# Two graph attention layers on one core: the first layer in seven row groups of 1024 and two of 512 instead of sixteen of 512

## The reference

```python
h = jnp.maximum(_layernorm(x, axis=-1), 0.0)
Wh = h @ W                                  # layer 1: h @ W.T
e = leaky_relu((Wh @ a1)[:, None] + (Wh @ a2)[None, :])     # slope 0.2
scores = jnp.where(adj > 0, e, -9e15)
x = x + elu(softmax(scores, axis=1) @ Wh)
```

## Time and profile before

| | us |
|---|---|
| median of the runs | 1394.34 |
| profiled execution | 1393.29 |
| its span on the core | 1391.6 |
| VectorE, ScalarE, TensorE busy | 1231.1, 1188.9, 1154.9 |

### The profile page before, as it was taken

How to read it: one execution, slowest core, us unless ns; L and a number is a source line. 1 busy time by engine, 2 the same in 40 slices (tenths; PEclk the granted TensorE clock), 3 DMA queues, 4 the chain that set the end, 5 groups by cost and what they waited for, 6 DMA issues and landing times.

```text
span 1391.6 us, 52932 instructions
## 1 busy us (share of the span) xinstructions
PE 1154.9 (83%) x20824; PEld 1121.6 (81%) x20824; DVE 1231.1 (88%) x2210; ACT 1188.9 (85%) x1826; POOL 312.8 (22%) x520
## 2 busy tenths in 40 slices
PE   2726989888898998998898660999899989999996
PEld 2525989888888898898898540999899989999996
DVE  6787889988999898999897778989899999998996
ACT  2346999999899999999999536799899989998995
POOL 2342454444444444444420000000000000000000
PEclk9857999999999999999999875999999999999998
DMA  9998999999999999999972100000101010110000
GB/s 157 168 209 148 212 198 208 212 211 189 211 204 212 211 210 211 209 211 211 210 142 55 27 2 32 2 25 2 33 2 32 2 33 8 27 33 2 17 2 24
DMA packets 128133, 157.09 MB, mean 113 GB/s; under 512 B 59280, under 2 KB 59408, under 8 KB 128016
## 3 DMA queue, kind: packets, MB, share of 16 engines
q0 software_dynamic: 73728, 134.25, 52.3%
q1 hardware_dynamic: 54288, 21.11, 6.9%
HBM read 285.25 MB, written 4.26 MB: 208 GB/s over the span
## 4 chain that ended last, share of the span: by engine, by line
PE 33%; issue 24%; DVE 19%; ACT 15%; DMA 8%; ACTq 1%; DVEq 1%; POOL 1%; POOLq 0%; SPq 0%
PE psum L1210 30%; ACT toggle L558 11%; DMA stream<-in_adj_dram 6%; DVE work L933 5%; DVE work L969 3%; DVE toggle L964 3%; ACT stream L575 2%; DVE stream L706 2%; PE psum L1105 2%; DVE toggle L946 1%; PE psum L1191 1%; DMA x_scratch<-y_tile 1%; ACT sums L575 1%; DVE work L813 1%; POOL stream L643 0%
## 5 line engine op out<-in xcount | busy, mean ns | idle before, releaser
L1210 PE MATMUL psum<-parts_d,toggle 128*128 128x130 f16 x8192 | 983.3, 223 | 40.6 <-DVE work L969 40.4
L1210 PE MATMUL psum<-parts_g,work 128*128 128x130 f16 x8192 | 983.1, 222 | 0.0
L1210 PEld LDWEIGHTS psum<-parts_d,toggle 128*128 128x128 fp8e4 x8192 | 804.7, 98 | 45.7 <-issue 45.3
L1210 PEld LDWEIGHTS psum<-parts_g,work 128*128 128x128 fp8e4 x8192 | 811.1, 99 | 5.6 <-issue 2.3
L558 ACT ACTIVATE toggle<-s_row,steep_d 128x512 uint8 (+1 forms) x952 | 590.8, 724 | 1.2 <-issue 0.2
L558 ACT ACTIVATE toggle<-stream,steep_d 128x1024 uint8<-128x1024 f32 x416 | 440.7, 1158 | 38.4 <-PE psum L1210 37.7
L643 POOL DMA_DIRECT2D stream<-in_adj_dram x512 | 311.5, 610 | 382.7 <-DVE stream L706 320.5
L964 DVE TENSOR_TENSOR toggle<-work,toggle 128x1024 int32<-128x1024 int32 x256 | 312.3, 1220 | 62.2 <-ACT toggle L558 59.2
L969 DVE TENSOR_TENSOR work<-work,toggle 128x1024 int32<-128x1024 int32 x256 | 311.7, 1218 | 0.7
L706 DVE TENSOR_SCALAR stream<-stream 128x1024 bf16<-128x1024 bf16 x512 | 201.8, 421 | 38.2 <-DMA stream<-in_adj_dram 30.9
L1105 PE MATMUL psum<-pack_w,stream 128*128 128x8 bf16 x4096 | 132.5, 166 | 73.4 <-DVE stream L706 68.6
(11 more groups left out here) (121 smaller groups left out, 361.7 us busy)
## 6 DMA issues: line engine op xcount, KB each, us to landing
stream<-in_adj_dram POOLq DMA_DIRECT2D x512, 256.0 KB, 7.6
s_row<-s_scratch SPq DMA_DIRECT2D x16, 256.0 KB, 6.1
stream<-s_scratch SPq DMA_DIRECT2D x8, 512.0 KB, 4.3
toggle<-in_x_dram SPq DMA_DIRECT2D x4, 512.0 KB, 6.9
x_tile<-in_x_dram SPq DMA_DIRECT2D x16, 128.0 KB, 10.6
x_scratch<-y_tile SPq DMA_DIRECT2D x16, 128.0 KB, 9.5
stream<-x_scratch SPq DMA_DIRECT2D x4, 512.0 KB, 5.4
stream<-x_scratch SPq DMA_DIRECT2D x8, 256.0 KB, 4.5
```

Of the source, the lines that this page charges most:

```text
L1210: ins = nc.tensor.matmul(psum[:, bank, COLS[third]:COLS[third + 1]], mask.bitcast(FP8), parts[e][:, t, :, :].rearrange("p k h -> p (k h)") ...
```

## The change

The first layer is cut into 7 groups of 1024 rows in 16 chunks, shaped as in the second layer, and 2 groups of 512 at its end. The code calls the three shapes K = 0, 1, 2. In the groups of 1024 ScalarE makes all four signs of a chunk; in the first small group VectorE takes one in every second chunk, in the second one in every chunk. 72 steps instead of 56 are converted ahead of the first group. The first six groups have 4 conversions a chunk as before, the seventh has 2 a chunk (32), the first small group 4 in each of its first six chunks (24). The sixteen pieces of a large group fill six PSUM banks and the words move to banks 6 and 7; no bank has a twin in K = 0, and the two small groups use three banks each. `take_sums` stands after chunk 2 everywhere. The tiles `s_row`, `sums`, `x_tile`, `y_tile` and `rden` are shared by both layers, and the total, tanh and exp tiles are parts of `sums`; so `take_sums` waits until y of the group before is written (`y_ready`), where it waited for the second step of the epilogue. `move` is cut in two, so that the load of a row of s can stand between. The code of the fallback for extreme inputs, which does not run here, is adapted.

```diff
-    GTS = (4, 8)
-    CTS = (8, 4)
+    GTS = (8, 4, 8)
+    LAYER_OF = (0, 0, 1)
+    COUNTS = (7, 2, 8)
+    CTS = (4, 8, 4)
-    AHEAD = 6 * PACE
+    AHEAD = 8
+    PACK_BANK = 6
...
-        return [s for s in range(AHEAD + c * PACE, AHEAD + (c + 1) * PACE) if s < limit]
+    def steps_at(K, g, c):
+        if K == 0 and isinstance(g, int) and g == COUNTS[0] - 1:
+            return list(range(AHEAD + 2 * c, AHEAD + 2 * c + 2))
+        if K == 0:
+            return list(range(AHEAD + c * PACE, AHEAD + (c + 1) * PACE))
+        if K == 1 and g == 0 and c < 6:
+            return list(range(AHEAD + 32 + c * PACE, AHEAD + 32 + (c + 1) * PACE))
+        return []
...
+    def own_tiles(K, g, c):
+        if K == 0:
+            return 0
+        if K == 1:
+            return int(g == 1 or c % 2 == 1)
+        return int(c % 4 != 3)
...
-                        for s in range(28 + 7 * i, 35 + 7 * i):
+                        for s in range(28 + 11 * i, 39 + 11 * i):
                             convert(0, s)
...
-                act.wait_ge(sums_free, g + (L * LGROUPS[0] + 1))
+                if not (isinstance(g, int) and gg == 0):
+                    act.wait_ge(y_ready, gg)
...
+                for c in range(CHUNKS[K]):
+                    signs(K, g, c, slot)
+                    for k in words_at(K, g, c):
+                        store_words(base_of(K, g), k)
+                    if before:
+                        if c == 2:
+                            take_sums(*before)
+                        if c == (13 if K != 1 else 6):
+                            tanh(*before[0:2])
...
+                        back = 2 if K == 2 and (bank < OWN_BANKS or bank >= 6) else 1
+                        pe.wait_ge(bank_free, g * BIG + (BEFORE[K] - (back - 1) * BIG + last_in_bank(K, bank, side) + 1))
```

More of the change, by code:

```diff
@@ L64, in gat2_kernel @@
     BLOCK = CTS[0] * GTS[0] * P
-    LAYER = (0, LGROUPS[0] * CHUNKS[0])
+    BIG = 8
     WPT = P // BITS
@@ L105, in own_tiles @@
[L105 to L120, removed]
@@ new lines, in own_tiles, with own_up_to, chunk @@
+    def own_tiles(K, g, c):
+        if K == 0:
+            return 0
+        if K == 1:
+            return int(g == 1 or c % 2 == 1)
+        return int(c % 4 != 3)
+    def own_up_to(K, g, c):
+        here = sum(own_tiles(K, g, k) for k in range(c + 1))
+        first = sum(own_tiles(1, 0, k) for k in range(CHUNKS[1]))
+        if K == 1:
+            return g * first + here
+        return g * sum(own_tiles(2, 0, k) for k in range(CHUNKS[2])) + (first + CHUNKS[1] + here)
+    def chunk(K, g, c):
+        return g * CHUNKS[K] + (CHUNK0[K] + c)
@@ L139, in gat2_kernel, with where, last_in_bank @@
+    def where(K, r, e, side):
+        q = 2 * r + e
+        if K == 1:
+            return 3 * side + q // 3, q % 3
+        if K == 2 and q < 3 * OWN_BANKS and side:
+            return q // 3 + 6, q % 3
+        return q // 3, q % 3
+    def last_in_bank(K, bank, side):
+        return max(r for r in range(GTS[K]) if bank in (where(K, r, 0, side)[0], where(K, r, 1, side)[0]))
     with ExitStack() as ctx:
@@ L586, in group @@
[L586 to L601 removed]
+                nc.scalar.activation(th[:, 0:gt, :], hneg[:, 0:gt, :], ACT.Tanh, scale=0.5)
@@ L1043, in between @@
-                        if not first:
-                            finish_between(L, g - 1, c, k)
-                    masks(L, g, c, between)
+                        for s in steps_at(K, g, c)[(0, 1, 2)[k]:(1, 2, PACE)[k]]:
+                            convert(base_of(K, g), s)
+                        if before:
+                            finish_between(K, c, k, before)
+                    masks(K, g, c, between)
             constants()
@@ L1194, in group @@
-            def group(L, g, limit, side=0):
-                for c in range(CHUNKS[L]):
-                    n = chunk(L, g, c)
-                    if L == 0:
-                        for s in steps_at(c, limit)[:2]:
-                            pack(g + 1, s)
+                    bank, third = where(K, r, e, side)
+                    if third:
+                        continue
+                    pieces = min(3, sum(where(K, k, f, side)[0] == bank for k in range(GTS[K]) for f in range(2)))
```

490 lines of the change are left out of this document (233 added, 257 removed).

## The result

The changed kernel takes 1443.56 us (median of 4 runs, 1438.0 to 1446.94) against 1394.67 for the kernel before in the same series: a ratio of 1.033, interval 1.025 to 1.041. It is slower by 3.3%. The prediction said 1408 us and 1391 to 1425, so it was wrong, by 36 us.

What follows compares the result with a forecast made beforehand. Loads at 211 GB/s were taken as the limit. Group 0 starting at 133.8 us, 510 for six big groups and 160.2 for the tail put the first layer's last copy at 804.0, +15 us: 1408 us, range 1391 to 1425.

Steps and rivals of the forecast that it cites:

- TensorE at the start of a big group: First layer, big groups: TensorE's busy 75.8 us plus 5.8 idle gives 81.6, under the loads' 84.5, so priced at nothing.
- the bank wait: At a big group's start the first seed waits for ScalarE's bank copies behind four signs: 5.8 us of TensorE idle.
- The margin of 3 us: In the six big groups, TensorE's 81.6 us with its idle time was held against 84.5 us for loads.
- The slow rival: First layer: TensorE becomes the limit through waits for bank copies; groups of 88 us, +39 us, 1432 us; chance 0.17.
- Its price for the clock, 1.8 us: After a boundary pause TensorE's clock is lower; a second slow chunk (5.42 us in place of 3.65) adds 1.8 us.
- The start: Before group 0: 16 more conversions and larger rows of s add 22.6 us; VectorE starts at 133.8, bounds 18 to 26.
- the 5.36 us without a releaser: Before group 0, after the last conversion: parts and seed, with 5.36 us without a releaser, were taken to stay.
- The figure from the loads' limit: Six big groups with loads: 17.8 MB each at 211 GB/s is 84.5 us, taken as 85.0, together 510 us.
- The tail: From VectorE's start of the seventh group to the first layer's last copy: ScalarE sets the pace, 160.2 us, bounds 155 to 166.
- The second layer: After the first layer: the second layer keeps its tiles and order and only changes addresses, so 0 us.
- Two bounds in the prediction's sum: Whole-kernel bounds of 1396 (start 18, groups 84.5, tail 156) and 1423 us (start 24, groups 86.3, tail 166).
- ScalarE's saved signs: Six big groups: ScalarE's sum falls by 7 us a group to 76.2, worth nothing while loads take 84.5.

Runs made afterwards that it cites:

- both edits: The changed kernel with TensorE's six looped big groups as straight code and bank copies behind chunk 1's signs, not chunk 2's: 1408.93 us, ratio 1.010.

## Why the prediction was wrong

**The step that failed** is the one about TensorE at the start of a big group: "75.8 us; with 5.8 it is 81.6, under 84.5. So I price it at nothing in the six groups, and the margin is 3 us." The size of the bank wait was right: 5.6 us of idle time, for 5.8, where nothing else holds TensorE. Priced at nothing it was 4.5 us off in six groups, as the runs with straight code show (516.9 us from VectorE's first unpack to that of the seventh group, against 512.4 with early copies). What the sum left out is that TensorE also waits for its own instructions. The loop body went from 768 products to 1536, and that is the larger part: 542.4 us with the loop, 516.9 without. Going back makes a gap of 5.9 us five times. It is not 5.9 us lost each time, since the bank wait lies under it; but it stands ahead of the packs, so that conversions and loads stop as well, the gaps within the groups, most of the larger ones 1.4 to 2.0 us, come on top, and after each gap the clock is at its lower level, 0.50 (1.2 GHz) from 314.2 to 322 us:

```profile
303.00:308.00 5.00, 5.00 (x114) 4.89 (x112) 5.00 (x12) 5.00 (x6) 1.06 (x2) 1.00 1.12 203
314.20:318.00 3.80, 3.37 (x36) 2.69 (x36) 3.03 (x4) 3.80 (x14) 1.05 (x2) 0.50 1.12 210
318.00:322.00 4.00, 2.48 (x20) 2.13 (x21) 0.00 (x0) 3.58 (x4) 0.00 (x0) 0.50 1.09 269
```

From the end of one group's packs (308.28) to the next packs behind chunk 0 (324.87) it is 16.6 us; with straight code and early copies 7.8 (302.98 to 310.80). A group of 90.4 us has TensorE busy for 77.5 and idle for 12.9; with both edits it is 85.4, 75.8 and 9.5. The margin of 3 us was a sum over data waits alone.

**The slow rival** said that TensorE would wait 6 us or more for copies at each boundary, with the lower clock behind it and under 205 GB/s in the groups. Its signs came, with groups of 90 us for its 88, except that the waits stood at the packs and were put down to issue or conversions and only once, at the seventh group, to copies. Its cause was there, but hidden: moving the copies alone gains nothing (1439.77). Its price for the clock, 1.8 us, was also too low for a pause of this length. It came from a chunk at a mean clock of 0.69 behind waits of 1.0 and 1.4 us; behind the gap of 5.93 us the first chunk runs from 314.84 to 324.87 us, 1.9 of them the second gap, where a chunk at full clock takes 3.65.

**The other steps.** The start came 6.2 us earlier than forecast: of the 5.36 us without a releaser in the earlier trace rows, which I had left standing behind the conversions, 1.23 are left. That is 4.1 of the 6.2 us; the rest was not taken apart. The figure from the loads' limit held: 512.4 us for 510 where the fetch is away, and there VectorE waits 51.0 us for loads (25.2 in the changed kernel). The tail was 163.3 us for 160.2, within its bounds. The second layer is 2.7 us longer, no more than the runs with the same loop there differ among themselves. Two bounds in the prediction's sum are not those of its parts (24 us for 26 at the start, 156 for 155 in the tail); with the parts' own it would run from 1395 to 1425, which changes nothing.

Once TensorE's loop is written out and the copies come earlier, the groups take 512.4 us for a forecast of 510: that shows which term was missing. That the whole forecast is met as well (1408.93 us, last copy at 803.8 for 804.0) is in part luck: a start 4.7 us too early makes up for 2.4 us in the groups and 2.2 in the tail.

Nothing was gained where the fetch is away either, as forecast: ScalarE's saved signs lie in groups that it does not set, and the start is still 16 us later.

## What to carry to other kernels

Before a loop body grows, count its instructions on each engine, and look in the DMA view of one pass for instruction packets: none means that the body is kept, and doubling it can make it too long to be kept. Here that made a gap of 6 us at each pass and, with what follows the gap, cost 4% (1452.94 us). When an engine's sum is held against another's with a margin of a few us, its own instruction supply belongs in the sum. Two waits that lie over each other hide each other: the copies gained nothing until the fetch was gone. A gap at the head of a loop is tested by its releaser's own end time and by moving the suspected releaser; a label alone is no proof.

## What the runs showed of the hardware

- TensorE kept a loop body of 768 products with weight loads and did not keep one of 1024. Going back to a body of 1536 that is not kept made a gap of 5.7 to 6.4 us in the first layer beside loads at 192 to 196 GB/s, and of 5.1 to 6.2 at 66 GB/s. With the body of 1024 it was 6.2 to 8.8 us, with the loads at 148 GB/s; why it was longer there stays open.
- In the second layer of the kernel before the same gap was 3.6 to 3.9 us, without packs at the head of the loop and with hardly any loads. Why it is shorter there stays open.
- After gaps of 5.7 to 6.0 us, with a second one of 1.6 to 1.9 us following, TensorE's clock was at its lower level (0.50) for 9 to 11 us three times and for 3 to 4 us twice (changed kernel); after waits of 5.4 to 5.7 us without a second gap, for 3 to 5 us (straight code). What decides between the short and the long stretch stays open.
- The profile put such gaps down to an earlier event, conversions or copies, in three of the five passes of the changed kernel and in the second layer.
- Straight code has no gap ahead of the packs at the head of the groups that had been passes of the loop, but beside saturated loads it has gaps of 0.4 to 2.6 us within it; in the kernel before, straight code costs 0.8%.
